# Rounding the attention matrix to its high part on VectorE instead of ScalarE, in a two-layer graph network

## The reference, cut to what matters

```python
h = maximum(layernorm(x), 0)
e = leaky_relu(sj[:, None, :] + si[:, :, None] + ab[0], 0.2)
t = A * exp(e)                                  # 1024 x 1024 per batch
t = t / (sum(t, axis=-1) + 1e-12)
H = h @ Wk[0] + t @ (h @ Wk[1]) + t @ t @ (h @ Wk[2]) + sum(bk)   # regrouped
x = x + relu(H)
h = maximum(layernorm(x), 0)
An = d(A + I) * (A + I) * d(A + I)              # d: 1 / sqrt of the row sum
x = x + relu(An @ h @ kernel + bias)
```

## Time and profile before

| what | value |
|---|---|
| median of three runs | 859.63 us |
| the profiled execution | 860.75 us |
| its span, first to last instruction | 858.0 us |
| mean granted TensorE clock | 0.996 of full speed |
| busy: PE, PEld, VectorE, ScalarE, POOL | 93%, 89%, 75%, 59%, 35% |

### The profile page before, as it was taken

One profiled execution on the slowest core, in us unless ns is written; L12 is line 12 of the kernel. 1 busy time (PEld: TensorE's weight loads), 2 busy tenths in 40 slices (PEclk: granted clock), 3 DMA queues, 4 the chain that ended last, 5 costly groups with the idle time before them and its releaser, 6 DMA issues.

```text
span 858.0 us, 15999 instructions
## 1 busy us (share of the span) xinstructions
PE 797.3 (93%) x6140; PEld 765.6 (89%) x6140; DVE 641.2 (75%) x1400; ACT 509.0 (59%) x997; POOL 300.3 (35%) x247
## 2 busy tenths in 40 slices
PE   4979999899989999899998999989998999989998
PEld 3869898899989999798998989989998999989998
DVE  4477697966978677985879759787687867787565
ACT  1597646766467564775647754576646756468232
POOL 1003234442263332631335323443325433163416
PEclk9998999999999999999999999999999999999999
DMA  5437242862347432674317734286243751256503
GB/s 184 172 123 221 87 135 68 254 219 92 107 141 245 158 124 70 200 237 166 129 37 216 252 104 136 62 251 228 66 132 119 234 201 46 91 176 202 190 23 99
DMA packets 65275, 128.70 MB, mean 150 GB/s; under 512 B 6320, under 2 KB 32304, under 8 KB 65200
## 3 DMA queue, kind: packets, MB, share of 16 engines
q1 hardware_dynamic: 54768, 93.86, 33.5%
q10 hardware_dynamic: 10432, 33.82, 13.3%
HBM read 119.28 MB, written 8.39 MB: 149 GB/s over the span
## 4 chain that ended last, share of the span: by engine, by line
PE 73%; DVE 15%; ACT 5%; issue 4%; POOL 1%; DMA 1%; SPq 0%; ACTq 0%; DVEq 0%
PE acc L984 17%; PE acc L986 16%; PE acc L985 16%; PE da L854 13%; PE db L854 6%; PE tp L846 3%; DVE a_raw L690 3%; DVE tg_e L647 3%; ACT t_hi L414 2%; DVE t_lo L651 2%; DVE z_tmp L702 2%; DVE o_tile L707 1%; POOL a_lo L311 1%; DVE ht_lo L608 1%; ACT tg_e L404 1%
## 5 line engine op out<-in xcount | busy, mean ns | idle before, releaser
L984 PE MATMUL acc<-g_hi,t_hi 128*128 128x256 f32 (+1 forms) x1024 | 293.1, 286 | 6.5 <-DVE g_tmp L665 5.2
L986 PE MATMUL acc<-g_hi,t_lo 128*128 128x256 f32 (+1 forms) x1024 | 290.1, 283 | 0.0
L985 PE MATMUL acc<-g_lo,t_hi 128*128 128x256 f32 x1024 | 288.9, 282 | 0.0
L311 POOL TENSOR_TENSOR a_lo<-a_raw,a_hi 128x512 fp32r<-128x512 f32 x128 | 186.3, 1474 | 177.3 <-ACT a_hi L455 175.7
L984 PEld LDWEIGHTS acc<-g_hi,t_hi 128*128 128x128 f32 x1024 | 194.2, 190 | 6.9 <-DVE g_tmp L665 5.5
L985 PEld LDWEIGHTS acc<-g_lo,t_hi 128*128 128x128 f32 x1024 | 194.6, 190 | 0.0
L986 PEld LDWEIGHTS acc<-g_hi,t_lo 128*128 128x128 f32 x1024 | 194.4, 190 | 0.0
L984 PE MATMUL acc<-g_hi,a_hi 128*128 128x256 f32 x512 | 147.3, 288 | 25.9 <-POOL a_lo L311 25.8
L985 PE MATMUL acc<-g_lo,a_hi 128*128 128x256 f32 x512 | 144.1, 281 | 0.0
L986 PE MATMUL acc<-g_hi,a_lo 128*128 128x256 f32 x512 | 143.9, 281 | 0.0
L404 ACT ACTIVATE tg_e<-si,sij 128x256 f32<-128x256 f32 x256 | 110.1, 502 | 25.1 <-DVE t_lo L651 25.1
(11 more groups left out here) (105 smaller groups left out, 1495.0 us busy)
## 6 DMA issues: line engine op xcount, KB each, us to landing
tg_a<-adj_t_dram ACTq DMA_DIRECT2D x64, 512.0 KB, 4.0
a_raw<-adj_dram SPq DMA_DIRECT2D x64, 512.0 KB, 4.1
a_raw<-adj_t_dram SPq DMA_DIRECT2D x64, 512.0 KB, 5.1
x_res<-x_dram SPq DMA_DIRECT2D x64, 128.0 KB, 3.5
out_dram<-o_tile SPq DMA_DIRECT2D x64, 128.0 KB, 3.2
h<-x_dram SPq DMA_DIRECT2D x7, 1024.0 KB, 5.5
h<-x_dram SPq DMA_DIRECT2D x4, 256.0 KB, 4.9
p<-wk_dram SPq DMA_DIRECT2D x1, 768.0 KB, 7.8
```

The source lines that it names most:

```text
L311: nc.gpsimd.tensor_tensor(a_half(a_lo, i, h), a_raw[:, i % RS, h * N // 2:(h + 1) * N // 2], a_half(a_hi, i, h).bitcast(F32), ALU.subtract ...
L984: nc.tensor.matmul(acc[:, s, 0:n], l_hi, r_hi, start=(jt == 0), stop=False)
L985: nc.tensor.matmul(acc[:, s, 0:D], l_hi, r_lo, start=False, stop=False)
L986: ins = nc.tensor.matmul(acc[:, s, 0:n], l_lo, r_hi, start=False, stop=(jt == NT - 1))
```

## The change

The rounding of T to `t_hi` moves from ScalarE's half-step (k, 1) to VectorE's, between the product and the subtraction. ScalarE still waits for the product there, because it issues the load that refills `tg_a`. VectorE takes over the wait for the matmuls that read the old `t_hi`, and waits on its own product before the copy and on its own copy before the subtraction.

```diff
@@ scalar engine, t_step
                 if half == 1 and k > 0:
                     u = k - 1
 
-                    if not first:
-                        act.wait_ge(acc_full, (b - 1) * PHASES + NT + 2 * (u // 2) + 2)
-
                     act.wait_ge(prod_ready, b * NU + u + 1)
-                    nc.scalar.copy(t_view(t_hi, u), tg_e[:, u % TS]).then_inc(t_hi_done, 1)
                     nxt = next_unit(b, u, last)
                     if nxt is not None:
                         load_t_unit(act, *nxt)
@@ vector engine, t_step
-                if half == 1 and k > 0 and u not in LOW_ON_POOL:
-
+                if half == 1 and k > 0:
+                    if b > 0:
+
+                        dve.wait_ge(acc_full, (b - 1) * PHASES + NT + 2 * (u // 2) + 2)
+                    dve.wait_ge(prod_ready, b * NU + u + 1)
+                    nc.vector.tensor_copy(t_view(t_hi, u), tg_e[:, s]).then_inc(t_hi_done, 1)
                     dve.wait_ge(t_hi_done, b * NU + u + 1)
                     nc.vector.tensor_tensor(t_view(t_lo, u), tg_e[:, s], t_view(t_hi, u).bitcast(F32),
                                             ALU.subtract).then_inc(t_ready, 1)
```

## The result

The changed kernel takes 877.52 us (median of 4 runs, 874.36 to 880.31), the kernel before 859.72 us. The ratio, estimated from all runs and not from the two medians, is 1.0201 with a 95% interval of 1.0162 to 1.0240: slower by about 2%, as forecast (873.5 us, range 858 to 881). The profiled execution is the shortest of the four, 874.36 us; two of them, at a mean granted clock of 0.98 where the others had 0.99, took 880.

The account below looks back on a forecast made before the run. TensorE, busy 93%, was taken as the bound. Stage Z +14, stage V +2 and start-up -2.2 make +13.8 on the profiled 860.75 us: 874.6; with the median 1.1 us lower, 873.5 us, range 858 to 881.

Parts of the forecast that it names:

- Where it is decided: Stage Z, where TensorE waits for `a_lo`, decides; VectorE, which gets the copy, is the fuller engine there (24.35 against 19.73 us).
- The copy's duration: VectorE's rounding of 1024 elements takes 0.71 us, at plain COPY's rate; upper bound 1.21 us.
- slow copy: Rival: slow copy without turns beside POOL; stage Z +6, stage V +5, 870 to 871 us; chance 0.26.
- Turns: Fast copy and POOL's subtraction run one after the other in stage Z, about 1.28 us a turn; chance 0.50.
- Steps 1 to 6: Stage Z followed part by part, from unit 2's copy to chunk 7: 2.0 us longer, seven times, +14 us.
- Step 1: Stage Z, unit 2: POOL's subtraction comes between copy and `t_lo`, so `t_lo` ends 1.9 us later.
- step 2: Stage Z: ScalarE's leaky ReLU of unit 4 waits; unit 3's diagonal and product run alone, saving 1.1 us each.
- Step 3: Stage Z: ScalarE, rid of `t_hi`, rounds chunk 5's first half earlier, a gain of about 1 us.
- step 6: Stage Z, chunk 7: unit 4's copy and `t_lo` stand in POOL's way; the chunk starts 2.0 us later.
- Stage V and the start-up: Two copies per batch in stage V spill 0.3 us, +2 us in all; quicker units in the start-up give -2.2 us.
- Waits for `a_lo` of 5 to 6 us per batch: Sign on TensorE: its waits for POOL's `a_lo` grow to 5 to 6 us per batch instead of 3.7.
- The clock: Rival: longer waits in stage Z lower the granted clock in each batch, adding some 24 us; 3 in 100.

Follow-up runs that it names:

- z_only: Kernel before, with the rounding on VectorE only for units 2 to 5 of all batches but the first (stage Z): 876.51 us, ratio 1.0203.
- not_z: Kernel before, with the rounding on VectorE everywhere except units 2 to 5 of all batches but the first: 858.34 us, ratio 0.9988.
- reduce_copy: Changed kernel, with VectorE's copy written as a sum over a last axis of one element: 870.14 us, ratio 1.0117 to the kernel before.
- start_u: Kernel before, with the rounding on VectorE only in the first batch and for units 6 and 7 of the others: 857.03 us, ratio 0.9973.

## Why the prediction was right, point by point

- **Where it is decided.** Right: `z_only` has the whole loss, `not_z` none of it. The wait on TensorE that moved along with the copy is not the cause: no copy of the changed kernel waits for TensorE.
- **The copy's duration.** 0.71 us forecast, 0.68 to 0.69 measured. The doubt about TENSOR_SCALAR was a misreading: one row at one size cannot tell a fixed cost from a rate. The "slow copy" rival rested on it and falls. The Trainium skill (VectorE: DVE Perf Modes, The perf-mode tier table) has copies and `tensor_scalar` in one tier; the trace agrees for both, with 0.55 ns per element for COPY and 0.53 for TENSOR_SCALAR.
- **Turns.** Right: 1.80 us beside POOL, 0.68 alone, and `reduce_copy`, with a longer copy that is not stretched, gets stage Z's loss back. The Trainium skill (SBUF — State Buffer, SBUF: two separate sides) says this of instructions in a two-port mode; the trace agrees, and a TENSOR_REDUCE of the same elements at 1.21 us shows the other side of it.
- **Steps 1 to 6.** In the times of before: `t_lo` of unit 2 ends at 248.22 (forecast 247.3). Step 1 was mis-sized: it counted one turn, and both the copy and `t_lo` paid one, so 2.8 us and not 1.9. The diagonal and product of unit 3 ran alone, as step 2 has it (0.28, 1.22), but the product ends at 250.43, where it ended before (forecast 250.1). Step 3's gain was 0.66 us at chunk 5, forecast as 1.0. `t_lo` of unit 3 ends at 256.03 (255.6), 3.2 us later than before where the forecast sign was 2 to 3; chunk 6 starts at 259.50 (259.1) and chunk 7 at 264.07 (263.75). In step 6 the copy of unit 4 did not stand in POOL's way: it ran alone (0.68 us) while POOL waited for `a_hi`, and only `t_lo` held POOL up. Stage Z grew by 2.3 us a batch; the forecast was 2.0.
- **Stage V and the start-up.** A batch grew by 2.55 us, so 0.25 outside stage Z (forecast: 0.3). From the first stage Z to the last product the seven batches cost 17.8 us; the forecast was 16. The first stage Z begins 3.25 us earlier (130.23 us, 133.48 before), where 2.2 were forecast. But 1.6 of the 3.25 are the first product's shorter wait, which is not the change's. Set against `z_only`, which has the start-up of the kernel before and that shorter wait too, and where the first stage Z begins at 132.47 us, the start-up gained 2.2 us, as forecast. The sum at the last product is +14.5 us (869.12 for 854.61); the forecast was +13.8.
- **Waits for `a_lo` of 5 to 6 us per batch.** Met where the clock stayed up: 1.35, 2.80 and 1.48 are 5.6 us in the batch shown, and as much in one other. Over all it was not met: 32.4 us are 4.6 per batch, in 18 waits and not 21. In the other five batches TensorE, at half speed (see below), reaches chunk 7 so late that the wait there is at most 0.27 us.
- **The clock.** That the longer waits make it fall in each batch had 3 chances in 100 and 24 us. It fell in five of seven, and the price was wrong: stage Z takes 31.12 to 31.23 us in those five, 31.10 and 31.11 us in the other two.
- **The median** lies 4 us above the forecast although the sum met the profiled execution (874.6 for 874.36). That meeting is partly luck: the batches cost 1.8 us more than forecast, and the first product's shorter wait gave 1.6 us back. The longer runs are those at the lower mean clock (0.98 for 0.99). But the kernel before, at 0.98, took 858.7 to 859.4 us, no longer than in its other runs, and the trace at hand is of the shortest run; what lengthens the others stays open.

## What to carry to other kernels

Before moving a step to an engine that shares paths with GpSimd, count the meetings in the stage where TensorE waits, not the busy time: 0.12 us more work in each copy cost nothing here, while the turns, and the buffer that came free late by them, carried the loss. Meetings elsewhere can be free: in stage U `t_lo` of units 6 and 7 takes 1.7 us and not 1.23 in `not_z` as in the changed kernel, and `not_z` loses nothing. A slower instruction that takes no turns can be the faster choice where a subtraction runs beside it, and the slower where nothing does. Put a moved step only where the trace shows the receiving engine waiting: the same copy gains in the start-up and loses in stage Z.

## What the runs showed that was not expected

In most batches TensorE's clock fell behind the wait of chunk 6. Two windows of the changed kernel, 4 us at the same place of two successive batches (length, busy PE, PEld, DVE, ACT, POOL, granted clock):

```profile
154.40:158.40 4.00, 4.00 (x23) 3.79 (x21) 3.93 (x5) 2.98 (x6) 3.11 (x3) 0.59 0.87 341
259.40:263.40 4.00, 2.62 (x23) 2.42 (x21) 3.93 (x5) 3.00 (x6) 3.12 (x3) 1.00 0.84 333
```

In the first, behind a wait of 2.81 us, the granted clock averages 0.59 (most of it at 1.2 GHz, the lower level); in the second, behind one of 2.80 us, it stays at 2.4 GHz. Of the seven such stretches five ran low. 23 products keep TensorE busy for 4.00 us in the one and 2.62 in the other, and VectorE, ScalarE and POOL are as busy in both: TensorE loses little, because it would have waited for `a_lo` of chunk 7 anyway: 1.48 us in the second batch, and in the first the timeline shows no wait there. Before, with waits of 2.10 us in stage Z, no stage Z of the profiled execution had such a stretch. But the length of the wait does not decide it: `start_u`, where that wait is 2.08 us, has one in all seven, and its batch is as long as before (102.30 us). One of them:

```profile
251.50:255.50 4.00, 4.00 (x21) 4.00 (x22) 3.97 (x6) 2.81 (x6) 3.12 (x3) 0.57 0.94 297
```

What decides it, and why two of the seven kept the full clock, stays open.
